# Cross attention with transposed scores: the maxima of a pair before the low halves of the next, output transfers in later iterations

## The reference, cut to what matters

```python
B, N, D = 4, 1024, 256; M, DC = 77, 192; H, DH = 16, 64
attn_in = adaln(x, cond, ...);   x = attn(attn_in, attn_in, sa_wq, ...) + x
cross_in = adaln(x, cond, ...);  ctx_n = ln(context, ...)
q = heads(cross_in @ ca_wq)                    # 16 heads of 64
k, v = split(ctx_n @ ca_wkv);  k, v = heads(k), heads(v)
q, k = rope(q), rope(k)
a = softmax(einsum('bhnd,bhmd->bhnm', q, k) * 64 ** -0.5)
x = einsum('bhnm,bhmd->bhnd', a, v) @ ca_wo + ca_bo + x
x = gelu(adaln(x, cond, ...) @ ff_w1 + ff_b1) @ ff_w2 + ff_b2 + x
```

## Time and profile before

| | us |
|---|---|
| median of 3 runs (lowest, highest) | 2480.38 (2478.98, 2482.85) |
| the profiled execution | 2478.87 |
| its span in the trace | 2477.1 |
| mean granted clock of TensorE | 0.941 |

### The profile page before, as it was taken

How to read it: one execution, slowest core, us unless ns; L and a number is a source line. 1 busy time by engine, 2 the same in 40 slices (tenths; PEclk the granted TensorE clock), 3 DMA queues, 4 the chain that set the end, 5 groups by cost and what they waited for, 6 DMA issues and landing times. The chain is left out here.

```text
span 2477.1 us, 40034 instructions
## 1 busy us (share of the span) xinstructions
PE 2228.5 (90%) x15036; PEld 1042.1 (42%) x15036; DVE 1860.5 (75%) x2924; ACT 1330.3 (54%) x1655; POOL 355.7 (14%) x201
## 2 busy tenths in 40 slices
PE   2499999999999999999999999944899999994899
PEld 2133333344333344333334333442465656563566
DVE  6579989877989886899986998574766666666453
ACT  5266666755676654666664666443443443444221
POOL 3100000000000000000000000023554545452000
PEclk9699999999999999999999999967898999986899
DMA  5101010101111011101010110052322222224211
GB/s 163 54 35 36 35 44 35 39 32 44 52 40 40 27 44 44 52 27 44 35 44 35 52 36 27 19 160 72 94 85 85 85 85 85 85 85 128 67 38 34
DMA packets 106254, 143.81 MB, mean 58 GB/s; under 512 B 28209, under 2 KB 74367, under 8 KB 106111
## 3 DMA queue, kind: packets, MB, share of 16 engines
q1 hardware_dynamic: 106111, 141.87, 17.9%
HBM read 55.70 MB, written 12.85 MB: 28 GB/s over the span
## 5 line engine op out<-in xcount | busy, mean ns | idle before, releaser
L642 PE MATMUL sa_ps_o<-sa_probs,sa_v_pair 128*64 128x512 f32 x2048 | 532.7, 614 | 2.9 <-DVE sa_mx L897 2.9
L806 ACT ACTIVATE sa_probs<-sa_ps_s 128x1024 f32<-128x1024 f32 x512 | 495.8, 1025 | 27.9 <-PE sa_ps_s L629 27.9
L897 DVE CUSTOM_DVE_ANT_0 sa_rise<-sa_ps_t,sa_rise 128x512 f32<-128x512 f32 x504 | 327.9, 688 | 190.7 <-PE sa_ps_t L606 190.3
L910 DVE TENSOR_TENSOR sa_acc<-sa_acc,sa_probs 128x1024 f32<-128x1024 f32 x384 | 462.6, 1246 | 7.2 <-ACT sa_probs L806 7.2
L794 ACT ACTIVATE sa_rise<-sa_ps_t 128x1024 f32<-128x1024 f32 x252 | 257.7, 1023 | 250.0 <-PE sa_ps_t L599 250.0
L642 PEld LDWEIGHTS sa_ps_o<-sa_probs,sa_v_pair 128*64 128x64 f32 x2048 | 101.9, 134 | 246.4 <-issue 173.7
L576 POOL TENSOR_TENSOR sa_xr<-sa_xr,sa_bo_row 128x1024 f32<-128x1024 f32 x8 | 21.6, 2726 | 1280.1 <-DMA sa_xr<-in_x 1280.1
L622 PE MATMUL sa_ps_s<-sa_hi 64*128 64x512 f16 x1024 | 194.5, 376 | 0.0
L622 PE MATMUL sa_ps_s<-sa_hi,sa_lo 64*128 64x512 f16 x1024 | 194.4, 376 | 0.0
L622 PE MATMUL sa_ps_s<-sa_lo,sa_hi 64*128 64x512 f16 x1024 | 194.4, 376 | 0.0
L629 PE MATMUL sa_ps_s<-sa_m_line,sa_m_ones 64*128 64x512 f16 x1024 | 189.5, 377 | 3.7 <-DMA sa_m_line<-sa_m_rows 3.7
(11 more groups left out here) (275 smaller groups left out, 4613.5 us busy)
## 6 DMA issues: line engine op xcount, KB each, us to landing
sa_swp<-sa_raw SPq DMA_DIRECT2D x128, 256.0 KB, 2.4
ca_swp<-ca_raw SPq DMA_DIRECT2D x70, 256.0 KB, 2.4
sa_inv<-sa_scratch SPq DMA_DIRECT2D x128, 128.0 KB, 2.9
ca_q_hl<-ca_hi SPq DMA_DIRECT2D x68, 128.0 KB, 2.3
ca_q_hl<-ca_lo SPq DMA_DIRECT2D x68, 128.0 KB, 2.3
sap_xs<-in_x SPq DMA_DIRECT2D x4, 1024.0 KB, 7.1
sa_xr<-in_x SPq DMA_DIRECT2D x4, 1024.0 KB, 5.9
cap_xs<-x_after_self SPq DMA_DIRECT2D x4, 1024.0 KB, 7.2
```

The lines of the kernel that those rows point to most:

```text
L642: ins = pe.matmul(ps_o[rows(x), half(c)], v_pair[:, kt, rows(x)], probs[:, kt % 2, c, half(x)], start=(kt == 0), stop=(kt == NK - 1))
L806: act.activation(probs[:, kt % 2, c, :], ps_s[c][:, :], ACT.Exp, scale=float(DH) ** -0.5).then_inc(s_p, 1)
L897: dve.tensor_tensor_reduce(out=larger, in0=max_banks(j, t)[:, half(x)], in1=larger, scale=1.0, scalar=-3.0e38, op0=ALU.add, op1=ALU.max, a ...
L910: dve.tensor_tensor(acc[:, c, :], before, probs[:, kt % 2, c, :], ALU.add).then_inc(s_acc[c], 1)
```

## The change

`project_context` no longer stacks the keys; their two halves stay where they are made (twelve transfers less). `cross_attention` is written anew and without loops:

- No stacking of queries either. Of a pair, TensorE forms first scores from the high halves alone, 16 matmuls of 64 rows by 77 columns, tokens on partitions (`bases`); VectorE takes all their maxima in one operation (`maxima`); a small transpose and ScalarE make a row of them (`row`), and SyncE lays them as a line (`line`).
- TensorE forms the scores once more in full, keys on the 77 partitions and 512 tokens along a row: 12 matmuls (`scores`), four for the maxima (`shift`); ScalarE takes the exponential straight from PSUM (`exponentials`); `values` and `totals` use its result as it stands. No transposes back.
- The values are evacuated undivided to `o_pair`, which has two buffers; sums, reciprocals and their spreading through DRAM as in the self attention; VectorE divides (`divide`), ScalarE and VectorE split (`high_output`, `low_output`) three iterations after the scores.
- The rotation is done by VectorE alone (`turned`). GpSimd is left with the bias of the output.
- The output projection of a batch runs two pairs into the next batch, at the end of iteration g = 10, 18, 26 (`output_batch`); the store of its tokens stands in SyncE's queue one iteration later and the load of the next tokens two. The last batch has its own ending.

The transfer moved behind the line and the inverses of the iteration after the output matmuls. The core of the diff (removed lines of `cross_attention` stand in the kernel above and are left out):

```diff
@@ -1041,14 +1038,7 @@
                 sp.dma_start(swp[0:P:2, half(n)], raw[1:P:2, half(n)]).then_inc(s_swap[n], 16)
                 sp.dma_start(swp[1:P:2, half(n)], raw[0:P:2, half(n)]).then_inc(s_swap[n], 16)
             for n in range(2):
-                sp.wait_ge(s_hi, n + 1)
-                for x in range(2):
-                    for dst in (k_hh[0:DH], k_hh[DH:P]):
-                        sp.dma_start(dst[:, half(n), x], hi[DH * x:DH * x + DH, half(n)]).then_inc(s_stack, 16)
-                sp.wait_ge(s_lo, n + 1)
-                for x in range(2):
-                    sp.dma_start(k_lo[:, half(n), x], lo[DH * x:DH * x + DH, half(n)]).then_inc(s_stack, 16)
-            sp.wait_ge(s_stack, 16 * 12)
+                sp.wait_ge(s_swap[n], 32)
...
+        hi = sb("hi", [P, 3, N], F16)
+        lo = sb("lo", [P, 3, N], F16)
         raw = sb("raw", [P, 2, N])
         swp = sb("swp", [P, 2, N])
+        probs = sb("probs", [M, 2, 2, N])
+        o_pair = sb("o_pair", [P, 2, N])
+        sums = sb("sums", [P, HALF])
+        few = sb("few", [P, 16])
+        inv = sb("inv", [P, N])
...
+        mx = sb("mx", [P, 2, 2 * TT])
+        m_rows = sb("m_rows", [2 * TT, P], F16)
+        m_line = sb("m_line", [P, N], F16)
+        m_ones = sb("m_ones", [P, P], F16)
+        ps_s = ps("ps_s", [P, 2, N])
         ps_o = ps("ps_o", [P, N])
+        ps_t = ps("ps_t", [P, N])
+        turn = [ps_t[:, 0:HALF], ps_t[:, HALF:N]]
...
+        def output_batch(g):
+            return g // PAIRS - 1 if PAIRS <= g < G and g % PAIRS == 2 else None
...
+            def line(j):
+                sp.wait_ge(s_mt_r, j + 1)
+                sp.dma_start(m_line[0:P:DH, :], m_rows[:]).then_inc(s_line, 16)
...
+                if 2 <= g < G:
+                    gather_sums(g - 2)
+                if g + 2 < G:
+                    swap(g + 2)
+                if g < G:
+                    line(g)
+                if 2 <= g < G + 2:
+                    spread_inverses(g - 2)
+                if g >= 1 and output_batch(g - 1) is not None:
+                    b = output_batch(g - 1)
+                    sp.wait_ge(s_yr, TT * (b + 1))
+                    sp.dma_start(y_v[b], xr[:]).then_inc(s_out, 16)
+                if g >= 2 and output_batch(g - 2) is not None:
+                    b = output_batch(g - 2)
+                    sp.wait_ge(s_out, 16 * (b + 1))
+                    sp.dma_start(xr[:], x_v[b + 1]).then_inc(s_x, 16)
...
+            def bases(g):
+                b, pair = g // PAIRS, g % PAIRS
                 for t in range(TT):
+                    at = t // 4 * HALF + t % 4 * M
+                    for x in range(2):
+                        ins = pe.matmul(ps_s[:, x, at:at + M],
+                                        hi[rows(x), g % 3, t * P:(t + 1) * P], k_hi[rows(x), pair, b, :],
+                                        start=True, stop=True)
+                ins.then_inc(s_base, 1)
...
+            def scores(g):
+                b, pair, s = g // PAIRS, g % PAIRS, g % 3
+                for c in range(2):
+                    for n, (k, q) in enumerate(((k_hi, hi), (k_lo, hi), (k_hi, lo))):
+                        for x in range(2):
+                            pe.matmul(ps_s[0:M, c, half(x)], k[rows(x), pair, b, :], q[rows(x), s, half(c)],
+                                      start=(n == 0), stop=False)
...
+            for g in range(G):
+                pe.wait_ge(s_hi, g + 1)
+                if g >= 1:
+                    pe.wait_ge(s_p, 2 * g)
+                bases(g)
+                if g + 3 < G:
+                    if g == 0:
+                        pe.wait_ge(s_q_r, 2 * 2 + 1)
+                    if g >= 2:
+                        pe.wait_ge(s_sum_r, g - 1)
+                    if output_batch(g - 1) is not None:
+                        pe.wait_ge(s_yr, TT * (output_batch(g - 1) + 1))
+                    project(g + 3, 0)
+                pe.wait_ge(s_max, g + 1)
+                pe.wait_ge(s_q_r, 2 * min(g + 3, G))
+                if output_batch(g - 1) is not None:
+                    pe.wait_ge(s_yr, TT * (output_batch(g - 1) + 1))
+                pe.transpose(turn[1][0:2 * TT, 0:P], mx[:, g % 2, :], ident[:, :]).then_inc(s_mt, 1)
+                pe.wait_ge(s_lo, g + 1)
+                scores(g)
+                if g >= 1:
+                    values(g - 1)
+                pe.wait_ge(s_line, 16 * (g + 1))
+                shift(g)
+                if g >= 1:
+                    if g + 3 < G:
+                        pe.wait_ge(s_q_r, 2 * (g + 3) + 1)
+                    elif g >= 2:
+                        pe.wait_ge(s_sum_r, g - 1)
+                    totals(g - 1)
+                if g + 3 < G:
+                    pe.wait_ge(s_mt_r, g + 1)
+                    project(g + 3, 1)
+                if output_batch(g) is not None:
+                    b = output_batch(g)
+                    pe.wait_ge(s_ot, PAIRS * (b + 1))
...
+            def evacuate_o(g, c):
+                act.wait_ge(s_pv, 2 * g + c + 1)
+                if g >= 2:
+                    act.wait_ge(s_ot, g - 1)
+                act.activation(o_pair[:, g % 2, half(c)], ps_o[:, half(c)], ACT.Copy).then_inc(s_oev, 1)
...
+            for g in range(G):
+                row(g)
+                if g + 3 < G:
+                    evacuate_q(g + 3, 0)
+                if g >= 3:
+                    high_output(g - 3)
+                for c in range(2):
+                    exponentials(g, c)
+                if g >= 1:
+                    evacuate_o(g - 1, 0)
+                    evacuate_o(g - 1, 1)
+                    evacuate_sums(g - 1)
+                if g + 3 < G:
+                    evacuate_q(g + 3, 1)
+                if g + 2 < G:
+                    high(g + 2)
...
+            def low_output(g):
                 dve.wait_ge(s_ohi, g + 1)
+                dve.tensor_tensor(o_lo[:, g % PAIRS, :], o_pair[:, g % 2, :], o_hi[:, g % PAIRS, :],
+                                  ALU.subtract).then_inc(s_ot, 1)
...
+            for g in range(G):
+                maxima(g)
+                if g + 1 < G:
+                    low(g + 1)
+                if g >= 3:
+                    divide(g - 3)
+                if g >= 2:
+                    reciprocals(g - 2)
+                if g + 2 < G:
+                    turned(g + 2)
+                if g >= 3:
+                    low_output(g - 3)
+                if output_batch(g) is not None:
+                    b = output_batch(g)
+                    dve.wait_ge(s_xb, 2 * (b + 1))
+                    for t in range(TT):
+                        residual(b, t)
```

More of the change, by code:

```diff
@@ L1242, in _ @@
[L1242 to L1255 removed]
+            pool.wait_ge(s_bo, 32)
@@ new lines, in totals, with output @@
+            def totals(g):
+                for c in range(2):
+                    for x in range(2):
+                        n = 2 * x + c
+                        ins = pe.matmul(turn[0][32 * n:32 * n + 32, :], ones32[0:M, 0:32], probs[:, g % 2, c, half(x)],
+                                        start=True, stop=True)
+                ins.then_inc(s_sum, 1)
+            def output(b, t, ks, start, stop):
+                ts = slice(t * P, (t + 1) * P)
+                return split_product(pe, y_bank(b, t), ks, (o_hi, o_lo), wo, lambda k: (slice(None), k, ts),
+                                     lambda k: (slice(None), k, slice(None)), start, stop)
@@ L1322, in _ @@
[L1322 to L1330 removed]
+            pe.wait_ge(s_init, 3)
```

464 lines of the change are left out of this document (203 added, 261 removed).

## The result

The changed kernel takes 2420.41 us (median of 4 runs, 2418.0 to 2424.61) against 2479.68 us (4 runs, 2477.38 to 2482.85): a ratio of 0.9762, 95% interval 0.9744 to 0.978. It is faster by 59 us. The forecast was 2398, 81 us less. The profiled execution took 2418.0 us, with a span of 2416.2.

What follows compares the result with a forecast made beforehand. It took a 10.35 us loop through VectorE and ScalarE as the bound. Stage end 1713.6 + 17.2 + 381 + 43 + 6 = 2160.8 against 2241.8, 81 us less, gave 2398 us; range 2362 to 2440.

Steps and rivals of the forecast that it cites:

- The loop of 10.35: Settled pair: VectorE's low to low_output, 7.25 us, then ScalarE's evacuations and high, 3.1 us, closed by the o_pair guard.
- The maxima lie in its idle part, which is what their early place brings.: VectorE's maxima, 1.4 us a pair, fall in idle time of the 10.35 us loop because they stand early.
- 20 intervals at 10.35: Cross attention's 20 settled intervals between maxima, 10.35 us each, 207 of the 381 us for all 31.
- The start: Stage starts at 1713.6, 6.4 us saved by dropping the stacking transfers; then 17.2 us to the first maxima.
- The bases: TensorE's 16 first-score matmuls of a pair: 0.9 us taken, 0.45 if row halves run side by side, 2.2 at mixed-tile pace.
- late for nobody: SyncE's queue has seven issues of 0.7 us, 5 us in a pair of 10, and delays no engine.
- hides entirely: Output transfer, placed later on SyncE's queue, costs nothing; its reload of xr has six pairs, 60 us, to land.
- SyncE would hold the next line back for the output matmuls, 21 us per batch: Cost on SyncE's queue if the output transfer did not have its later place: 21 us per batch.
- The tail: From the last maxima to the stage's end: 40 us, plus 3 for TensorE restarting at 1.2 GHz.
- B: Rival: o_pair's guard doesn't bind, operations overlap more, and TensorE's order sets 9.1 us a pair; 2364 us; chance 0.13.
- C: Rival: TensorE's clock falls as often as now or more; 2432 us at 0.8, 2458 at 0.75; chance 0.18.
- E: Rival: a transfer decides, the line landing 6 us after the row instead of 2.6; 12.2 us a pair, 2458; chance 0.06.

Runs made afterwards that it cites:

- the tightened kernel: Changed kernel with three buffers for o_pair, the bias add on VectorE in the output iteration, and SyncE's swap issued ahead of the gather: 2373.53 us.

## Why the prediction was right, and where it was off

The direction, the bound and the loop were right; the gain was forecast 22 us too large, of which the profiled execution accounts for 20: +1.1 and +1.8 at the start, +21.7 in the intervals, +2.3 in the tail, less the 6 that were added for the clock, less 0.8 in what follows the stage.

- **The loop of 10.35.** Right: 10.32 from low to low, with the two waits that were named, VectorE's before low (34.3 us in 25 places) and ScalarE's before evacuate_o (48.4 in 21). Taking its guard away gave 29.5 us.
- **"The maxima lie in its idle part, which is what their early place brings."** Right in kind and too small: behind low they cost 59 us, 31 by the longer loop and 27.5 by the clock, which falls after TensorE's wait in it. Without this order the rest of the change is worth nothing: 2479.0 against 2479.6 us.
- **20 intervals at 10.35.** This is the term that was mis-sized: 11.4 on average, 21 us. The three pairs beside GpSimd's add are 12.8 over (14.5 + 14.5 + 14.9 - 3 x 10.35), six more at a granted clock of 0.74 to 0.85 are 8.1 over, the two of 12.1 with a late swap 3.5, and the other nine 3.8 under. These are not independent: the stop of TensorE behind a pair lengthened by the swap or by GpSimd is the longer one (3.9 and 6.3 us, against 2.1 behind a pair of 10.3), and with the add taken away the same three pairs still took 11.7, 11.7 and 12.7.
- **GpSimd's bias add.** The prediction had no term for it, because the add stands beside the path. The trace of before had the row to see it by: VectorE's 1024-wide add takes 3.35 us, not 1.22, while GpSimd works (timelines of VectorE and of GpSimd before the change):

```profile
1730.88 3.35 DVE L1394 TENSOR_TENSOR ca_rot<-ca_rot,ca_swp 128x1024 f32<-128x1024 f32 x1 [18.73 <-POOL ca_swp L1229]
```

```profile
1730.80 2.34 POOL L1227 TENSOR_TENSOR ca_rot<-ca_raw,ropeC 128x1024 f32<-128x1024 f32 x1
```

  That delay is GpSimd's 2.34 less the 0.08 between the starts, and then VectorE's own 1.1: 3.35. In the changed kernel, with 2.34 for each of the two adds, it is the same: 1898.19 + 2.34 is 1900.53, and 1.15 more is 1901.68; L1460 ends at 1901.69. VectorE waits for GpSimd's whole instruction. The Trainium skill, SBUF — State Buffer, section "Who interferes with whom", says that a VectorE instruction with two SBUF inputs contends with a GpSimd instruction that reads SBUF, that the lock is exclusive and the order of issue decides who blocks, and that a reduction never contends. The first two agree with these rows. So does the third: in the kernel with the maxima behind low, GpSimd's adds run from 1917.11 to 1923.72, and the maxima within that time take their usual 1.43 us, while the divide behind them takes 2.01 instead of 1.22 (timeline of VectorE):

```profile
1918.15 1.43 DVE L1472 TENSOR_REDUCE ca_mx<-ca_ps_s 128x16 f32<-128x1232 f32 x1
1919.50 2.01 DVE L1481 TENSOR_TENSOR ca_o_pair<-ca_o_pair,ca_inv 128x1024 f32<-128x1024 f32 x1
```

- **The start.** The context stage ends 1.1 us later than forecast (first issue of the stage at 1714.71 instead of 1713.6; 1719.94 before), so 5.2 of the 6.4 us came. From there to the first maxima it takes 18.96 for 17.2; the bias add on VectorE brings these maxima 3.7 earlier.
- **The bases.** 0.9 taken, 0.46 measured for all 16. That is the 0.45 of the prediction's case of two row halves side by side.

```profile
1892.04 0.46 PE L1271 MATMUL ca_ps_s<-k_hi,ca_hi 64*128 64x77 f16 x16
```

  In the changed kernel it gained nothing: its pace is that of the other loop, where ScalarE's high, from 1894.91 for 1.08 us in its timeline above, ends later than the bases. With three buffers it shows, as 8.7 where the forecast had 9.1.
- **SyncE "late for nobody", and the transfer that "hides entirely".** Both wrong. VectorE waits 22.0 us in 13 places for the swap, 9.4 of them in eight of the settled pairs; and the load in pieces gave 10 us in the tightened kernel. "SyncE would hold the next line back for the output matmuls, 21 us per batch" failed in size and in mechanism: 9.4, by the store's landing and the load ahead of the line.
- **The tail.** 45.3 us from the last maxima for 43.
- **The rivals.** B, the guard that doesn't bind, is refuted by its own waits, and its 2364 was about what the kernel could do once guard and add were gone (2375). C, the clock, came half true. The forecast expected fewer falls: from 1740 to 2060 the granted clock rose from 0.90 to 0.94, but over the stage it is 0.90 as before, since it is 0.79 up to the first maxima and 0.77 in the tail. Of C's sign the pace above 11 showed (11.4), the clock under 0.85 did not. Its price was also summed wrongly: by its own 8.0 us that scale, a clock of 0.8 gives 0.75 a pair and not 0.6, and twice 20 x 0.6 is 24, not 34. The rule of the Trainium skill that the prediction weighed (TensorE: Matmul & The Clock Gate, "A second HAM failure mode: psum-queue depth-cycling"), short idles that make the clock swing, agrees with the two kernels that have low ahead of the maxima (clock 0.87, and 0.97 with the wait filled); in the changed kernel it did not bring the 2432 of that case. E in its form (the line) did not happen; a transfer that decides did, for the swap.

## What to carry to other kernels

Price a loop that is closed by a guard by its whole path over all engines, and then look at what an engine with a clock gate does in the wait that is left: here most stops of TensorE of 2.5 to 4 us in the pairs had slow matmuls behind them, so moving one 1.4 us instruction was worth 59 us. Work "off the path" on GpSimd, or one large transfer, is free only if it holds up nothing on the path; look for one row of the trace in which an instruction beside it takes longer than its kind. A third buffer of 4 KB a partition was the cheapest change of all.

## What the runs showed of the hardware that was not expected

- VectorE's 1024-wide product with both inputs in SBUF takes 1.8 to 3.4 us beside GpSimd's add of the same size, 1.22 alone; two GpSimd adds block for 3.2 us more in the pair around 1900. VectorE's maxima over PSUM keep their 1.43 us beside such an add.
- Adding ten matmuls (2.15 us by 0.215 each) to a wait of TensorE made a kernel 27 us faster, at a granted clock of 0.97 instead of 0.87.
- Sixteen matmuls of 64 rows, 128 columns of weights and 77 moving columns take 0.46 us in all, 0.03 each, while matmuls with mixed tile heights went 0.14 apart before the change.
- A transfer of 8 KB took 4.4 us from its issue to its reader's start when it was issued 3.3 us behind one of 1 MB, with a swap between them.
